# Expert passes of two half-filled experts in place of one, in a vision-transformer kernel

## The reference, cut to what matters

```python
h = gelu(einsum('nd,edm->nem', xf, W1) + b1)      # d = 192, m = 768, e = 32
y = einsum('nem,emd->ned', h, W2) + b2
out = einsum('ne,ned->nd', comb, y)               # comb: four weights per token, the rest 0
```

## Time and profile before

| | |
|---|---|
| three timed runs | 329.39, 331.78 (median), 339.75 us |
| profiled execution | 333.88 us, of it 331.8 us from the first to the last instruction |
| mean granted TensorE clock | 0.962 of full speed |
| TensorE busy | 306.9 us (93%) |
| VectorE, ScalarE, GpSimd busy | 141.0, 107.0, 85.7 us |
| moved by DMA | 54.32 MB, mean 164 GB/s |

### The profile page before, as it was taken

How to read it: one execution, slowest core, us unless ns; L and a number is a source line. 1 busy time by engine, 2 the same in 40 slices (tenths; PEclk the granted TensorE clock), 3 DMA queues, 4 the chain that set the end, 5 groups by cost and what they waited for, 6 DMA issues and landing times.

```text
span 331.8 us, 7359 instructions
## 1 busy us (share of the span) xinstructions
PE 306.9 (93%) x2730; PEld 259.8 (78%) x2731; DVE 141.0 (43%) x423; ACT 107.0 (32%) x300; POOL 85.7 (26%) x96
## 2 busy tenths in 40 slices
PE   8899996999999999999999999991989799979994
PEld 6868975899899999999999999991957687445553
DVE  0664758345343333323232332110249666545554
ACT  1246233043243323333233332341033564501110
POOL 4500000514434344443444545312115000000000
PEclk9999999699999999999999999997679999979999
DMA  7990048108778787787777887701400000000001
GB/s 274 396 385 5 4 129 362 35 7 283 242 257 298 278 272 265 286 310 265 254 275 286 308 270 236 287 21 40 160 0 3 2 4 0 0 0 2 0 0 47
DMA packets 11986, 54.32 MB, mean 164 GB/s; under 512 B 3585, under 2 KB 4934, under 8 KB 7472
## 3 DMA queue, kind: packets, MB, share of 16 engines
q1 hardware_dynamic: 8400, 49.03, 40.3%
q0 software_dynamic: 3264, 3.69, 4.6%
q10 hardware_dynamic: 288, 1.14, 0.9%
HBM read 53.71 MB, written 4.26 MB: 175 GB/s over the span
## 4 chain that ended last, share of the span: by engine, by line
PE 82%; DVE 9%; issue 3%; DMA 2%; ACT 2%; SPq 1%; DVEq 0%
PE ps L945 20%; PE ps L908 14%; PE ps L918 9%; PE ps L1016 4%; PE ps L1004 4%; PE ps L728 3%; PE ps L898 3%; PE ps L650 3%; DMA attn_rows<-in_attn_rows 2%; PE ps L1007 2%; PE ps L971 2%; PE ps L890 2%; PE ps L735 1%; PE ps L715 1%; PE ps L813 1%
## 5 line engine op out<-in xcount | busy, mean ns | idle before, releaser
L618 ACT ACTIVATE turned<-ps,route_in 128x128 f32<-128x128 f32 x204 | 56.1, 372 | 98.7 <-PE ps L918 78.2
L945 PE MATMUL ps<-expert_w,turned 128*128 128x192 f32 x408 | 72.0, 327 | 0.0
L945 PEld LDWEIGHTS ps<-expert_w,turned 128*128 128x128 f32 x408 | 65.5, 190 | 0.2
L467 POOL DMA_INDIRECT x_rows<-xn_rows,row_ids x34 | 35.1, 1031 | 95.0 <-DVE row_ids L1206 94.1
L908 PE MATMUL ps<-fexp,expert_w 128*128 128x128 f32 x408 | 51.2, 275 | 0.4 <-DVE fexp L1209 0.4
L908 PEld LDWEIGHTS ps<-fexp,expert_w 128*128 128x128 f32 x408 | 49.9, 192 | 0.6 <-issue 0.6
L479 POOL DMA_INDIRECT y_picks<-fexp,row_ids x34 | 35.3, 1038 | 46.3 <-DVE fexp L1299 39.1
L1299 DVE COPY fexp<-ps 128x192 f32<-128x192 f32 x34 | 12.2, 358 | 47.4 <-PE ps L945 45.5
L918 PE MATMUL ps<-fexp,expert_w 64*128 64x128 f32 x408 | 31.9, 289 | 0.0
L918 PEld LDWEIGHTS ps<-fexp,expert_w 64*128 64x128 f32 x408 | 25.4, 187 | 4.3 <-issue 0.4
L1206 DVE TENSOR_TENSOR row_ids<-ps,cst 128x2 uint32<-128x2 f32 x34 | 5.4, 159 | 51.6 <-PE ps L898 51.2
(11 more groups left out here) (221 smaller groups left out, 365.6 us busy)
## 6 DMA issues: line engine op xcount, KB each, us to landing
expert_w<-in_experts SPq DMA_DIRECT2D x34, 1152.0 KB
ffn<-in_ffn_in SPq DMA_DIRECT2D x1, 2592.0 KB, 10.6
probsT<-in_patches SPq DMA_DIRECT2D x4, 384.0 KB, 7.2
qk_padT<-y_picks SPq DMA_DIRECT2D x4, 384.0 KB, 4.5
attn_in<-in_attn_in SPq DMA_DIRECT2D x1, 864.0 KB, 5.2
attn_w<-in_attn_w SPq DMA_DIRECT2D x1, 673.5 KB, 9.0
wtokT<-in_tok_w ACTq DMA_DIRECT2D x1, 576.0 KB, 5.1
x_rows<-xn_rows,row_ids POOLq DMA_INDIRECT x34
```

The costliest lines, as they stand in the source:

```text
L467: pool.indirect_dma_start(out=x_rows[:, x_u, :], out_offset=None, in_=xn_rows, in_offset=bass.IndirectOffsetOnAxis(ap=row_ids[:, u % STEPS ...
L618: last = act.activation(hidden[:, u % 2, c, :], ps[:, 2 + 2 * (u % 2) + c // 3, (c % 3) * P:(c % 3 + 1) * P], ACT.Gelu, bias=b1T[:, c, bas ...
L945: last = nc.tensor.matmul(ps[:, 6 + u % 2, 0:D], hidden[:, u % 2, c, :], w2[:, u % RING, c, :], start=(c == 0), stop=(c == KH - 1))
```

## The change

A pass now holds 64 slots of each of two experts. There are 16 home passes (experts 2u and 2u+1) and overflow passes of two 64-slot tiles each, which may belong to different experts. The number of overflow passes is worked out on VectorE; with these inputs there are 16 further tiles of 64 tokens (12 experts with one, two with two), so 8 overflow passes, and 24 passes in all.

- **First layer by slot, then turned.** `up_in` now has the slots standing in the array (64 columns for each expert, in the left and the right half) and streams the weights through: four matmuls of 384 columns over 128 rows (two column halves x two experts), and four of 384 columns over 64 rows for the tail. The result has the slot on the partition. VectorE copies it, 128x768, to `raw` (`raw_out`), and TensorE turns it in six transposes (`turn_raw`) at the end of the step, behind the second layer of u. ScalarE takes the gelu in two halves, 12 instructions of 128x64, since each expert has its own bias.
- **Second layer.** Twelve matmuls of 64 standing columns and 192 streamed ones, the two experts in the two column halves, waiting for each half of the gelu by itself.
- **Ids.** Eight matmuls of 64 standing columns in place of four of 128. In overflow passes VectorE first copies the row codes of the two experts (`ov_codes`).
- **Eight expert buffers**, four pairs: four in `expert_w`, three over the place of layer 1's weights (`late_in`), one in `probs`. A pair is 2 x 1152 KB, and its load still waits for the second layer four passes earlier. Eight experts instead of four are loaded at the start.
- **Layer 1's weights** are loaded late: `attn1_in` after the last second layer, ahead of the wait for the scatters and of the read-back; `ffn1_in` behind the read-back.
- The counts of further tiles are worked out with a comparison against seven thresholds and a sum, in place of a chain of comparisons.

The diff, cut to its core:

```diff
-NOV = (TOK * PICKS) // P - 1
+SLOTS = 64
+PAIR = P // SLOTS
...
-ROUNDS = NE // STEPS
-OV_ROUNDS = -(-NOV // STEPS)
-OVPAD = (OV_ROUNDS + 1) * STEPS
+PASSES = NE // PAIR
+ROUNDS = PASSES // STEPS
+MORE = TOK // SLOTS - 1
+OV_PASSES = (TOK * PICKS) // P
+NOV = OV_PASSES * PAIR
+OV_ROUNDS = OV_PASSES // STEPS
+OVPAD = (OV_ROUNDS + 1) * STEPS * PAIR
+W1_COLS = HID + HID // 2
+W_COLS = W1_COLS + KH * D
...
-                  ("before", P), ("earlier", EG), ("place", P),
+                  ("before", P), ("earlier", EG), ("place", SLOTS),
...
+        attn1_in, ffn1 = late_in[:, 0:9 * D], late_in[:, 9 * D:]
         w13T = ffn1[:, 0:2 * N1 * P].rearrange("p (e m d) -> p e m d", e=N1, m=2)
...
+        ov_codes = sb("ov_codes", [P, 2, PAIR, NT, 2], F16)
...
+        expert_w = sb("expert_w", [P, 4 * W_COLS])
+        after_probs = probs[:, :, :, :].rearrange("p t h k -> p (t h k)")
+        weights = [expert_w[:, n * W_COLS:(n + 1) * W_COLS] for n in range(4)] + [late_in[:, n * W_COLS:(n + 1) * W_COLS] for n in range(3)] + [after_probs[:, 0:W_COLS]]
+        w1 = [w[:, 0:HID] for w in weights]
+        w1_tail = [w[:, HID:W1_COLS] for w in weights]
+        w2 = [w[:, W1_COLS:].rearrange("p (c d) -> p c d", c=KH) for w in weights]
+        raw = after_probs[:, W_COLS:W_COLS + HID]
...
-            def load_expert(e, u, done):
-
-                sp.dma_start(expert_w[:, u, :], dram["experts"][bass.ds(e, 1), :, :].rearrange("a p n -> (a p) n")).then_inc(done, 16)
+            def load_pair(i, ov_round, u):
+
+                for q in range(PAIR):
+                    e = expert_of(sp, i, ov_round, u, q)
+                    sp.dma_start(weights[u % RING * PAIR + q], dram["experts"][bass.ds(e, 1), :, :].rearrange("a p n -> (a p) n")).then_inc(w_dma[u % RING], 16)
...
             for u in range(RING):
-                load_expert(u, u, w_dma[u])
+                load_pair(0, None, u)
...
-            sp.dma_start(attn1_in[:, :], dram["attn1_in"]).then_inc(attn1_dma, 16)
-            sp.dma_start(ffn1[:, :], dram["ffn1_in"]).then_inc(ffn_dma, 16)
...
-                            load_expert(expert_of(sp, i, ov_round, u + RING), u % RING, w_dma[u % RING])
+                            load_pair(i, ov_round, u + RING)
 
+            sp.wait_ge(down_mm, tiles + PASSES)
+            sp.dma_start(attn1_in, dram["attn1_in"]).then_inc(attn1_dma, 16)
...
+            sp.dma_start(ffn1, dram["ffn1_in"]).then_inc(ffn_dma, 16)
...
                     with where_tile(act, tiles, ov_round, u):
-                        act.wait_ge(up_mm, tile + 1)
...
-                        for c in range(KH):
-                            last = act.activation(hidden[:, u % 2, c, :], ps[:, 2 + 2 * (u % 2) + c // 3, (c % 3) * P:(c % 3 + 1) * P], ACT.Gelu,
-                                                  bias=b1T[:, c, bass.ds(tile, 1)])
-                        last.then_inc(gelu_done, 1)
+                        for half in range(2):
+                            act.wait_ge(rawT_mm, 2 * tile + half + 1)
+                            if first and u in COMB_STEPS:
+                                at = P * (2 * COMB_STEPS.index(u) + half)
+                                act.copy(combT[:, at:at + P], ps[0:NE, 4 + half, 3 * P:4 * P]).then_inc(combT_sb, 1)
+                            for c in range(KH // 2):
+                                for q in range(PAIR):
+                                    last = act.activation(hidden[:, u % 2, half * (KH // 2) + c, slots_of(q)], ps[:, 4 + half, c * P + q * SLOTS:c * P + (q + 1) * SLOTS],
+                                                          ACT.Gelu, bias=b1T[:, half * (KH // 2) + c, bass.ds(tile * PAIR + q, 1)])
+                            last.then_inc(gelu_done, 1)
...
-                one = bass.ds(expert_of(pe, i, ov_round, step), 1)
                 for t in range(NT):
-                    last = nc.tensor.matmul(ps[:, b, 2 * P:2 * P + 2], onehot[:, b, t, :], row_codes[:, t, one, :], start=(t == 0), stop=(t == NT - 1))
+                    for q in range(PAIR):
+                        codes = ov_codes[:, b, q, t] if is_overflow(ov_round, step) else row_codes[:, t, expert_of(pe, i, ov_round, step, q)]
+                        last = nc.tensor.matmul(ps[slots_of(q), b, 2 * P:2 * P + 2], onehot[:, b, t, slots_of(q)], codes, start=(t == 0), stop=(t == NT - 1))
...
-            def up_in(i, u, first=False):
-
-                buf, w_u = u % 2, u % RING
-                pe.wait_ge(w_dma[w_u], 16 * (i * (STEPS // RING) + u // RING + 1))
+            def up_in(i, u):
+
+                buf, w_u = u % 2, u % RING * PAIR
+                pe.wait_ge(w_dma[u % RING], 16 * PAIR * (i * (STEPS // RING) + u // RING + 1))
                 pe.wait_ge(rowsT_sb, i * STEPS + u + 1)
                 for half in range(2):
-                    for c in range(KH // 2):
-                        nc.tensor.matmul(ps[:, 2 + 2 * buf + half, c * P:(c + 1) * P], w1[:, w_u, (c + 3 * half) * P:(c + 3 * half + 1) * P],
-                                         x_rowsT[:, buf, 0, :], start=(c == 0), stop=False, skip_group_check=True)
+                    for q in range(PAIR):
+                        nc.tensor.matmul(ps[slots_of(q), 2 + half, 0:HID // 2], x_rowsT[:, buf, 0, slots_of(q)],
+                                         w1[w_u + q][:, half * (HID // 2):(half + 1) * (HID // 2)], start=True, stop=False, skip_group_check=True)
+                for q in range(PAIR):
+                    for half in range(2):
+                        rows = slice(half * DB, (half + 1) * DB)
+                        last = nc.tensor.matmul(ps[slots_of(q), 2 + half, 0:HID // 2], x_rowsT[rows, buf, 1, slots_of(q)],
+                                                w1_tail[w_u + q][rows, :], start=False, stop=True, skip_group_check=True)
+                last.then_inc(up_mm, 1)
+
+            def turn_raw(i, u, first=False):
+
+                pe.wait_ge(raw_sb, i * STEPS + u + 1)
                 if first and u in COMB_STEPS:
                     pe.wait_ge(comb_ready, 1)
-                    for half in range(2):
-                        nc.tensor.matmul(ps[0:NE, 2 + 2 * buf + half, 3 * P:4 * P], comb[:, 2 * COMB_STEPS.index(u) + half, :], ident,
-                                         start=False, stop=True, skip_group_check=True)
-                for c in range(KH // 2):
-                    for half in range(2):
-                        rows = slice(half * DB, (half + 1) * DB)
-                        last = nc.tensor.matmul(ps[:, 2 + 2 * buf + half, c * P:(c + 1) * P], w1_tail[rows, w_u, c * P:(c + 1) * P],
-                                                x_rowsT[rows, buf, 1, :], start=False, stop=True, skip_group_check=True)
-                last.then_inc(up_mm, 1)
+                for half in range(2):
+                    if first and u in COMB_STEPS:
+                        nc.tensor.transpose(ps[0:NE, 4 + half, 3 * P:4 * P], comb[:, 2 * COMB_STEPS.index(u) + half, :], ident)
+                    for c in range(KH // 2):
+                        at = (half * (KH // 2) + c) * P
+                        last = nc.tensor.transpose(ps[:, 4 + half, c * P:(c + 1) * P], raw[:, at:at + P], ident)
+                    last.then_inc(rawT_mm, 1)
 
...
-                            up_in(i, u + 1, first)
+                            up_in(i, u + 1)
...
-                        pe.wait_ge(gelu_done, i * STEPS + u + 1)
-                            last = nc.tensor.matmul(ps[:, 6 + u % 2, 0:D], hidden[:, u % 2, c, :], w2[:, u % RING, c, :], start=(c == 0), stop=(c == KH - 1))
+                            if c % (KH // 2) == 0:
+                                pe.wait_ge(gelu_done, i * (2 * STEPS) + 2 * u + c // (KH // 2) + 1)
+                            for q in range(PAIR):
+                                last = nc.tensor.matmul(ps[slots_of(q), 6 + u % 2, 0:D], hidden[:, u % 2, c, slots_of(q)], w2[u % RING * PAIR + q][:, c, :],
+                                                        start=(c == 0), stop=(c == KH - 1))
                         last.then_inc(down_mm, 1)
+                        with where_tile(pe, tiles, ov_round, u + 1):
+                            turn_raw(i, u + 1, first)
...
+            turn_raw(0, 0)
             tiles = rounds(pe, experts)
-            pe.wait_ge(y_ready, tiles + NE)
-
...
                 if is_overflow(ov_round, step_):
-                    ins = dve.scalar_tensor_tensor(out=onehot[:, b], in0=ov_place[:, :, one].to_broadcast([P, NT, P]),
-                                                   scalar=const("ov_first")[:, bass.ds(ov_round * STEPS + step_, 1)], in1=where, op0=ALU.subtract, op1=ALU.is_equal)
+                    where = place16[:, :].unsqueeze(1).to_broadcast([P, NT, SLOTS])
+                    for q in range(PAIR):
+                        one = bass.ds(expert_of(dve, i, ov_round, step_, q), 1)
+                        dve.tensor_copy(ov_codes[:, b, q].unsqueeze(2), row_codes[:, :, one, :])
```

(41 more changed lines are left out.)

45 lines of the change are left out of this document (15 added, 30 removed).

## The result

| us | before | after |
|---|---|---|
| median, lowest to highest of 4 runs | 332.32, 329.39 to 339.75 | 323.18, 320.79 to 324.14 |
| profiled run, span | 333.88, 331.8 | 324.14, 322.3 |

The account below looks back on a forecast made before the run. DMA at 6.2 us a pass was taken to bound the expert stage, just over TensorE's 5.9. Stage -14.6, late `attn1_in` +0.5 and colder picks +1.5 sum to -12.6: median 331.78 to 319 us, range 309 to 337.

Parts of the forecast that it names:

- TensorE's pass: Expert stage: TensorE needs 5.9 us for a pass of two experts, against 4.63 for one; 24 passes for 34.
- overlap of tiles: TensorE's pass: column halves run beside each other, 1.8 to 2 times, and small tiles more than two at once.
- six changes, 0.8: TensorE's pass: six changes of the array's division at 0.1 to 0.16 us each, against two before; 0.8 us taken.
- Rivals 2: Expert stage: array changes and tail quarters make TensorE the bound at 7.3 us a pass, 353 us in all; chance 0.14.
- 3 (9.7): Expert stage: column halves do not overlap with long streams, 9.7 us a pass, 412 us in all; chance 0.04.
- DMA's pass: Expert stage: two experts' weights at 423 GB/s take 5.6 us, gathers and scatters 0.64; 6.2 us a pass.
- Rival 1: Expert stage: mixed transfers stay at 353 GB/s, 7.1 us a pass, end at 336 us; chance 0.19.
- the covers: Each pass: ScalarE's gelu (2.8 us) and VectorE's `raw_out` (at most 958 ns) stay hidden behind TensorE's work.
- the stage: Expert stage, from the first up at 64.93 us: ends near 210 us instead of 224.6, a gain of 14.6.
- pairs 0 to 3 came in the idle DMA time of the first attention: Before the expert stage: the eight early expert loads cost nothing, and the first up still starts at 64.93 us.
- The 6.56 us in which nothing is shown are no prize: End of the stage: the read-back, not the skipped steps, releases the picks, so this stretch stays; nothing gained.
- layer 1 "unchanged": Layer 1, behind the picks: takes the same time as before, a term of 0.

Follow-up runs that it names:

- the repeat: The changed kernel, unaltered, executed again: median 325.52 us, ratio to the kernel before 0.9847.
- late pairs: The changed kernel with pairs 2 and 3 of the early expert loads issued behind the writing of the token rows: 317.47 us, and 315.50 us when run again.
- the run with two steps: The kernel before, with TensorE's overflow round cut from eight guarded steps to two: 329.44 us, ratio 0.9870.

## Why the prediction was right, and where it was not

**Right: TensorE's pass.** Forecast 5.9 us, measured 5.74. The step that carried it, overlap of tiles read from lines 692, 701 and 745, held with 384 columns: eight up records in 1.44 us are 180 ns each, where the price of 0.84 ns a column gives one alone 322, so two ran at a time; the quarters took 0.81 where 0.65 for four at a time and 1.29 for two stood open, so four ran. Each part but ids lies 0.14 to 0.16 us over its pure stream (1.29, 0.65, 0.21, 1.95, 0.66), 0.76 together, which was the term "six changes, 0.8". And where the tail was left out, ids followed up in the same division of the array and took 0.10 us instead of 0.22. The rule of "TensorEngine Tiling (Array Packing)" in the Trainium skill, section Tiling Modes, that a change of mode drains the engine, fits this, with a price here of 0.12 to 0.16 us each. Rivals 2 (7.3 us) and 3 (9.7) are out.

**Right: DMA's pass.** From pass 0's end at 86.21 to up(23) at 211.91 the last 20 pairs took 125.7 us; 125 and 1 of landing were forecast. Between 423 GB/s (loads alone) and 353 (mixed, at full share) the measurement decides: 414 GB/s over 100 us. That the fuller queue is the reason, as the prediction argued, was not tested by itself. Rival 1 is out. The 358 GB/s of the Trainium skill, "DMA: Bandwidth & Descriptors", section Bandwidth, is not what this core got; the same section has 425 GB/s for one core whose neighbour is idle, and that agrees better with the 414. Gathers and scatters cost less than taken, 3.4% of 322.3 = 11.0 us of all engines against 15.3, with fewer packets for the same bytes.

**Right: the covers.** ScalarE's 12 instructions took 2.56 us (2.8 forecast), and TensorE waited for the gelu once, 1.2 us at the last pass, where the forecast had it, and once, 0.9, for `raw`. `raw_out` took 957 ns.

**Two us short: the stage.** 147.04 us for 145.1. The piece from the first up to pass 0's end took 12.48 for 10.2: in this execution its second layer ran at half clock, 3.78 us where the repeat has 2.10. In the repeat the piece took 10.80, as with late pairs, and its whole stage 145.4 (74.81 to 220.25): the forecast of the stage holds for an execution whose pass 0 runs at full clock.

**Wrong: the start, by 8.8 us.** The failed step is "pairs 0 to 3 came in the idle DMA time of the first attention", costed at nothing. The cover was named and was real, DMA was idle there; but what the loads could disturb was not asked. They take 2.4 us from TensorE directly and most of the rest through the clock.

**Wrong: the end, by 4 us the other way.** The failed step is "The 6.56 us in which nothing is shown are no prize". I took the read-back for what released the picks and passed over the 965 matmuls between the skipped steps and them; and I took the time of the read-back as fixed. In after the 965 matmuls run at 221.3 to 222.6, under the scatter, and the read-back is issued 4.6 us behind the stage's end instead of 5.7. The picks start 7.9 us behind it, 3.2 sooner than in before; the run with two steps had 4.0, of which 2.0 are the 965 matmuls and 2.0 an earlier read-back. Against it stood what was forecast: picks colder by 1.0 (1.5 taken), and `attn1_in` beside the scatter, which costs 1 us or more where 0.5 was taken.

**Wrong: layer 1 "unchanged", by 3.5 us in the profiled pair.** It is the same work, at another clock where the two can be told apart (0.65 for 1.28 us). Why is open, so this step failed without a known cause.

So +8.8 was missed on one side and 4.2 + 3.5 on the other; with the 2 us of the stage the sum ended 3 us low. That it is so near is luck: it looks better than its steps. Without the miss at the start, as in the kernel with late pairs (315.5 to 317.5 us), the change is worth 0.955 to 0.96.

## What to carry over

Halving padding by pairing experts pays as long as the tiles overlap, but it doubles the bytes per pass, so the gain ends where the loads meet TensorE's period; compute both, since taking work off either one then gives little (5.5 and 3.3 us of 146 here). Idle DMA time is not free time: before filling it, look whether TensorE runs a long straight piece of program there, and put bulk loads behind it if their data isn't needed yet. An "issue" gap is worth costing as a gain when another piece of work stands between it and the next thing that is awaited; compare when that thing lands with when the waiting engine is through with the other piece.

## What the runs showed of the chip

- Bulk loads at a share of 1.00 to 1.03 (421 to 425 GB/s) beside straight-line TensorE work gave a pause of 2.16 to 2.43 us at the same record in three executions of two kernels, and 0.50 of clock for 12 us and more behind it; with the first up 8.8 to 9.9 us later than in the earlier trace rows. With half of these loads 20 us later the first up came at 64.86 to 66.77 us in seven executions, and it comes at 64.42 to 65.87 in three of the old kernel.
- A packet of the instruction queues moved 1 to 2.4 us later than in other executions went with a pause of 0.26 to 2.43 us behind the 117th record, which ended 2.4 to 2.7 us behind the packet in all five executions that have it.
- Layer 1's first matmuls ran at half clock in every execution of a kernel built on the old one and in three of those built on the new one (without the tail, and the two with `attn1_in` later), not in the other six. The cause is open.
- An indirect scatter of one tile lands in 2.1 to 2.2 us alone and in 3.2 to 4.6 us beside an 864 KB load that was issued 1.3 us before it.
